# A gated cross-attention and mixture-of-experts block: a new order in the tail, and all expert numbers of a block table loaded by TensorE ahead of its blocks

## The reference

```python
def attn(q, kv, mask):                      # q = layernorm(x), kv = ctx
    qh, kh, vh = heads(q @ Wq.T), heads(kv @ Wk.T), heads(kv @ Wv.T)
    p = softmax(einsum('bhqd,bhkd->bhqk', qh, kh) + mask)
    return concat(einsum('bhqk,bhkd->bhqd', p, vh)) @ Wo.T

def ffn(x):                                 # x = layernorm(x)
    shared = (silu(x @ shared_gate.T) * (x @ shared_up.T)) @ shared_down.T
    probs = sigmoid(x @ router_w.T + routing_bias)          # 8 experts
    scores, idx = top_k(probs, 2); scores /= scores.sum(-1, keepdims=True)
    w = zeros(tokens, 8).at[idx].add(scores)
    g, u = silu(einsum('th,ehi->tei', x, gate_w)), einsum('th,ehi->tei', x, up_w)
    return shared + einsum('tei,eih,te->th', g * u, down_w, w)   # inner size 256

x = x + tanh(g_xattn) * attn(layernorm(x), ctx, mask)
x = x + tanh(g_ffn) * ffn(layernorm(x))
```

## Time and profile before

| | us |
|---|---|
| median of 3 runs | 206.19 (205.8 to 206.8) |
| the profiled execution, whole | 207.47 |
| its span, from the first to the last instruction | 204.9 |

### The profile page before, as it was taken

How to read it: one execution, slowest core, us unless ns; L and a number is a source line. 1 busy time by engine, 2 the same in 40 slices (tenths; PEclk the granted TensorE clock), 3 DMA queues, 4 the chain that set the end, 5 groups by cost and what they waited for, 6 DMA issues and landing times.

```text
span 204.9 us, 4737 instructions
## 1 busy us (share of the span) xinstructions
PE 169.0 (82%) x1400; PEld 141.6 (69%) x1400; DVE 133.6 (65%) x622; ACT 110.2 (54%) x402; POOL 110.6 (54%) x146
## 2 busy tenths in 40 slices
PE   7498798899998999989999685897498999999300
PEld 7386577888798987889987574786377776776200
DVE  2486997649895767767687686367565565665124
ACT  4368889178674586783688531435243554654100
POOL 5079889727976055784445986324314455555600
PEclk9999999999999999999999999579799999999955
DMA  5999971800000000010000100120011122131054
GB/s 154 315 385 394 353 297 41 326 0 16 2 3 13 5 0 14 30 39 3 0 0 5 41 13 13 43 62 31 28 44 52 52 69 57 43 86 34 18 151 156
DMA packets 12583, 17.35 MB, mean 85 GB/s; under 512 B 2011, under 2 KB 8929, under 8 KB 12432
## 3 DMA queue, kind: packets, MB, share of 16 engines
q1 hardware_dynamic: 10160, 14.28, 20.6%
q0 software_dynamic: 1312, 2.26, 3.8%
q10 hardware_dynamic: 1088, 0.52, 0.9%
HBM read 10.01 MB, written 7.51 MB: 85 GB/s over the span
## 4 chain that ended last, share of the span: by engine, by line
PE 54%; DVE 17%; DMA 9%; issue 7%; POOL 6%; ACT 4%; SPq 1%; ACTq 0%; POOLq 0%
PE misc L379 7%; PE o_bank L368 6%; PE s_even L343 5%; PE pt L353 4%; PE proj_k L620 4%; DVE probs L873 3%; DMA wq_raw<-wqT 3%; PE proj_q L300 3%; DMA ys<-probsT,xg 3%; POOL ys L1357 3%; PE proj_k L300 2%; DMA probs<-ys 2%; PE proj_q L302 2%; PE proj_q L301 2%; PE proj_k L302 2%
## 5 line engine op out<-in xcount | busy, mean ns | idle before, releaser
L672 ACT ACTIVATE probs<-probs,negmax 128x128 f32<-128x128 f32 x128 | 49.9, 392 | 9.1 <-DVE negmax L873 9.1
L1255 POOL TENSOR_TENSOR probs<-probs,rinv 128x512 f32<-128x512 f32 x32 | 32.9, 1040 | 28.1 <-DVE rinv L887 28.0
L1357 POOL DMA_INDIRECT ys<-probsT,xg x23 | 22.6, 983 | 25.5 <-ACT probsT L802 16.8
L672 ACT ACTIVATION_READ_ACCUMULATOR probs<-probs,negmax 128x1 f32 x128 | 24.2, 189 | 0.0
L873 DVE CUSTOM_DVE_ANT_0 probs<-s_even,mask 128x128 f32<-128x128 f32 x64 | 17.9, 279 | 4.4 <-issue 4.4
L343 PE MATMUL s_even<-kT,qT 64*128 64x128 f32 x128 | 18.4, 284 | 2.9 <-issue 2.9
L1285 POOL DMA_INDIRECT xs<-xrow,slot x16 | 16.1, 1005 | 8.1 <-issue 4.7
L620 PEld LDWEIGHTS proj_k<-down_sb,v 128*128 128x128 f32 x92 | 12.1, 190 | 10.6 <-issue 10.6
L343 PEld LDWEIGHTS s_even<-kT,qT 64*128 64x128 f32 x128 | 15.4, 187 | 5.1 <-issue 4.4
L620 PE MATMUL proj_k<-down_sb,v 128*128 x92 | 16.2, 299 | 2.9 <-DVE v L1192 2.4
L343 PE MATMUL s_odd<-kT,qT 64*128 64x128 f32 x128 | 18.5, 285 | 0.0
(11 more groups left out here) (236 smaller groups left out, 455.7 us busy)
## 6 DMA issues: line engine op xcount, KB each, us to landing
xs<-pad SPq DMA_DIRECT2D x5, 858.0 KB, 5.6
xg<-xs SPq DMA_DIRECT2D x23, 66.0 KB, 1.9
down_sb<-down SPq DMA_DIRECT2D x1, 1152.0 KB, 8.8
gu_raw<-gu SPq DMA_DIRECT2D x3, 256.0 KB, 7.0
wk_raw<-wkT SPq DMA_DIRECT2D x2, 256.0 KB, 4.7
wq_raw<-wqT SPq DMA_DIRECT2D x2, 256.0 KB, 6.7
mask<-mask SPq DMA_DIRECT2D x8, 64.0 KB, 2.2
wv_raw<-wvT SPq DMA_DIRECT2D x2, 256.0 KB, 7.1
```

Of the source, the lines that this page charges most:

```text
L672: e = act.activation(probs[:, r, l, :], probs[:, r, l, :], ACT.Exp, bias=negmax[:, r, l:l + 1], scale=-1.0, accum_out=rowsum[:, r, l:l + 1])
L1255: pool.tensor_tensor(quad, quad, rinv[:, r, 4 * u:4 * u + 4].unsqueeze(2).to_broadcast([P, 4, P]), ALU.mult).then_inc(norm_done, 1)
L1357: pool.indirect_dma_start(out=ys, out_offset=bass.IndirectOffsetOnAxis(ap=xg[n % IN_FLIGHT][:, P:P + 1].bitcast(U32), axis=0), in_=y_sb[n ...
```

## The change

It has these parts, all behind the attention of batch 5 except where a line says otherwise.

- TensorE's order: `transposes(15)` ahead of `gate_up(0, 0)`; `out_project(7)` directly behind `values(15)`, ahead of `logits(3)` and `gate_up(0, 1)`; `down_step(0)` into the first block; `gate_up(1, 0)`, `gate_up(1, 1)` into the last block and `down_step(1)` behind it.
- The block loop is cut in two, `blocks(0, EARLY)` and `blocks(EARLY, BLOCKS)`. A part ends with its last `block_down` before the next one begins. The second waits for the second table, which VectorE now makes (`table_steps(1)`) after the first block's `add_shared(0)`.
- All `block_expert` loads of a part stand at its head: five ahead of block 0, 18 ahead of block 5.
- The first half of the shared expert takes silu as tanh (`gate_tanh` on ScalarE and two operations of VectorE, `gate_hidden`).
- `choose_steps` finds the experts with `max_index`; its chain is five steps shorter to follow and has no scan.
- GpSimd splits the weights of the last experts and spreads the scatters at other places; `scatter(2)` comes ahead of `count_chosen(2)`.
- `ys` is laid out so that a token's two rows are neighbours; four loads of 256 KB take the place of eight of 128 KB, and SyncE and ScalarE store two parts each.
- PSUM banks are given out anew for this.

```diff
-        g_bank, u_bank = [s_bank[0], pt_bank[0]], [s_bank[1], pt_bank[1]]
-        d_bank = [proj_bank["k"], proj_bank["q"]]
-        route_bank = [misc, misc, proj_bank["q"], proj_bank["q"], proj_bank["q"]]
+        g_bank = [[s_bank[0], pt_bank[0]], [o_bank, s_bank[0]]]
+        u_bank = [[s_bank[1], pt_bank[1]], [misc, s_bank[1]]]
+        d_bank = [pt_bank[1], proj_bank["q"]]
+        route_bank = [misc, misc, proj_bank["q"], proj_bank["q"], proj_bank["k"]]
         x2_cols, lg_cols, rk_cols = slice(P, 3 * P), slice(384, 400), slice(400, 416)
         cnt_cols = slice(416, 424)
-        tx_bank, hT_bank, y_bank = [o_bank, misc], pt_bank, proj_bank["k"]
+        tx_bank, hT_bank, y_bank = [o_bank, misc], pt_bank[0], pt_bank[1]
...
+        y_rows = probs.rearrange("p r l k -> p (r l) k")[:, 0:B * TOP_K, :]
+
+        def load_y(engine, n):
+            part = slice(2 * TOP_K * n, 2 * TOP_K * (n + 1))
+            engine.dma_start(y_rows[:, part, :], ys.rearrange("(p r) h -> p r h", p=P)[:, part, :]).then_inc(in_y[n], 16)
+
+        def store_out(engine, n):
+            tiles = slice(2 * n, 2 * n + 2)
+            engine.wait_ge(sum_ready, n + 1)
+            engine.dma_start(out[:, tiles, :], x_sb[:, tiles, :]).then_inc(out_sem, 16)
 
...
-                load_y(sp, n, 0)
-            for n in range(4):
-                tiles = slice(2 * n, 2 * n + 2)
-                sp.wait_ge(sum_ready, n + 1)
-                sp.dma_start(out[:, tiles, :], x_sb[:, tiles, :]).then_inc(out_sem, 16)
+            load_y(sp, 0)
+            load_y(sp, 2)
+            store_out(sp, 0)
+            store_out(sp, 2)
...
             transposes(14, 2)
             out_project(B - 2, use)
             values(14, last, 2)
+            pe.wait_ge(ez_ready, 3)
             ranks(2)
+            transposes(15, 3)
             pe.wait_ge(gulo_ready, EXPERTS)
             pe.wait_ge(ttr_done, 8 * GROUPS)
             gate_up(0, 0)
-            transposes(15, 3)
             x2_transposes(3)
             values(15, last, 3)
+            out_project(B - 1, use + 1)
             logits(3)
             gate_up(0, 1)
-            out_project(B - 1, use + 1)
+            x2_transposes(LAST)
+            pe.wait_ge(ez_ready, 4)
             ranks(3)
-            pe.wait_ge(in_down, 16)
-            down_step(0)
-            x2_transposes(LAST)
             logits(LAST)
-            pe.wait_ge(h_done, 1)
-            gate_up(1, 0)
-            pe.wait_ge(h_done, 2)
-            gate_up(1, 1)
-            pe.wait_ge(ez_ready, LAST + 1)
-            ranks(LAST)
 
 
             def block_expert(n):
                 late = n >= EARLY
-                if n == 0 or n == EARLY:
-                    pe.wait_ge(table_ready, 1 + late)
                 row = n - EARLY * late
                 return pe.value_load(table[late][row:row + 1, 1:2], min_val=0, max_val=E_ROUTED)
 
...
-                    pe.wait_ge(h_done, 3)
+                    pe.wait_ge(h_done, 1)
...
-                if n >= 2:
-                    pe.wait_ge(hidT_ready, n - 1)
+                if n:
+                    pe.wait_ge(hidT_ready, n)
                 else:
-                    pe.wait_ge(h_done, 4)
+                    pe.wait_ge(h_done, 2)
                 for c in range(2):
-                    mm = pe.transpose(hT_bank[n % 2][:, c * P:(c + 1) * P], hid[n % 2][:, c * P:(c + 1) * P], ident_sb[:])
...
+            def blocks(first, end):
+
+                experts = {n: block_expert(n) for n in range(first, end)}
+                block_transpose(first)
+                block_transpose(first + 1)
+                block_gate_up(first, experts[first])
+                for n in range(first, end):
+                    if n + 2 < end:
+                        block_transpose(n + 2)
+                    if n + 1 < end:
+                        block_gate_up(n + 1, experts[n + 1])
+                    if n == BLOCKS - 1:
+                        pe.wait_ge(xglo_ready, BLOCKS)
+                        gate_up(1, 0)
+                    if n > first:
+                        block_down(n - 1, experts.pop(n - 1))
+                    elif not first:
+                        pe.wait_ge(in_down, 16)
+                        down_step(0)
+                    block_hidden_transpose(n)
+                    if n == BLOCKS - 1:
+                        pe.wait_ge(hid_ready, BLOCKS)
+                        gate_up(1, 1)
+                block_down(end - 1, experts[end - 1])
+
+            pe.wait_ge(ez_ready, LAST + 1)
+            ranks(LAST)
+            pe.wait_ge(table_ready, 1)
+            blocks(0, EARLY)
+            pe.wait_ge(table_ready, 2)
+            blocks(EARLY, BLOCKS)
+            pe.wait_ge(counts_read, 2)
+            down_step(1)
...
+            def gate_tanh(c):
+                act.wait_ge(gu_done, c + 1)
+                act.activation(silu_sb[:, c, :], g_bank[0][c][:], ACT.Tanh, scale=0.5).then_inc(silu_done, 1)
+
+            def silu(c):
+                act.wait_ge(gu_done, c + 3)
+                act.wait_ge(h_done, c + 1)
+                act.activation(silu_sb[:, c, :], g_bank[1][c][:], ACT.Silu).then_inc(silu_done, 1)
...
+                    if n == BLOCKS - 1:
+                        silu(0)
+                block_y(end - 1)
+
+            blocks(0, EARLY)
+            blocks(EARLY, BLOCKS)
+            silu(1)
             for i in range(IN_FLIGHT):
                 act.wait_ge(y_out[i], 16 * len(range(i, BLOCKS, IN_FLIGHT)))
-            for n in range(4):
-                load_y(act, n, 1)
+            load_y(act, 1)
+            load_y(act, 3)
+            store_out(act, 1)
+            store_out(act, 3)
...
+                for i, b in enumerate(ROUTED[r]):
+                    dve.max_index(chosen_at[:, b, :], top[:, b, :], prob[:, i, :]).then_inc(route_step, 1)
...
+            def gate_hidden(c):
+                dve.wait_ge(silu_done, c + 1)
+                dve.scalar_tensor_tensor(silu_sb[:, c, :], silu_sb[:, c, :], 1.0, g_bank[0][c][:], ALU.add, ALU.mult).then_inc(gate_done, 1)
+                dve.wait_ge(gate_done, c + 1)
+                dve.scalar_tensor_tensor(h_sb[:, 0, c, :], silu_sb[:, c, :], 0.5, u_bank[0][c][:], ALU.mult, ALU.mult).then_inc(h_done, 1)
+
+            def hidden(c):
+                dve.wait_ge(silu_done, c + 3)
+                dve.tensor_tensor(h_sb[:, 1, c, :], silu_sb[:, c, :], u_bank[1][c][:], ALU.mult).then_inc(h_done, 1)
...
-            mask_max(15, PAIRS - 1, 3, after(6, copy_o, 13, 1))
-            x2_lo(2)
+            mask_max(15, PAIRS - 1, 3, chain(after(2, x2_lo, 2), after(5, copy_o, 13, 1)))
             recips(15, 3, (0,))
             copy_pt(14, 2)
-            finish(choose_steps(2))
+            choice = choose_steps(2)
+            run(choice, 3)
             recips(15, 3, (1,))
+            finish(choice)
             add_attention(B - 2, use)
+            norm = norm2_steps(B - 2, use)
+            run(norm, 2)
+            finish(weight_steps(2))
             copy_o(14, 2)
-            steps = norm2_steps(B - 2, use)
-            run(steps, 2)
-            finish(weight_steps(2))
             place(2)
-            block_table(0)
+            first_table = table_steps(0)
+            run(first_table, 1)
             copy_pt(15, 3)
-            finish(steps)
+            finish(norm)
             copy_o(15, 3)
             x2_lo(3)
-            hidden(0, 0, 0)
-            finish(choose_steps(3))
-            hidden(1, 0, 1)
+            finish(first_table)
             add_attention(B - 1, use + 1)
-            steps = norm2_steps(B - 1, use + 1)
-            run(steps, 2)
+            norm = norm2_steps(B - 1, use + 1)
+            run(norm, 2)
+            choice = choose_steps(3)
+            run(choice, 4)
+            finish(norm)
+            finish(choice)
             finish(weight_steps(3))
-            finish(steps)
+            x2_lo(LAST)
             place(3)
-            x2_lo(LAST)
-            add_shared(0)
+            gate_hidden(0)
             finish(choose_steps(LAST))
             finish(weight_steps(LAST))
-            hidden(2, 1, 0)
-            place(LAST)
-            hidden(3, 1, 1)
-            block_table(1)
 
             def block_lo(n):
                 dve.wait_ge(xghi_ready, n + 1)
...
+            def blocks(first, end):
+
+                block_lo(first)
+                block_lo(first + 1)
+                if not first:
+                    place(LAST)
+                    gate_hidden(1)
+                block_hidden(first)
+                for n in range(first, end):
+                    if n > first:
+                        block_hidT(n - 1)
+                    if n + 2 < end:
+                        block_lo(n + 2)
+                    if n + 1 < end:
+                        block_hidden(n + 1)
+                    if n == 0:
+                        add_shared(0)
+                        finish(table_steps(1))
+                    if n == BLOCKS - 1:
```

(84 more changed lines are left out.)

105 lines of the change are left out of this document (29 added, 76 removed).

## The result

The changed kernel takes 215.84 us in the median of four runs (214.11 to 217.28), the kernel before 206.5 in the same comparison. The ratio is 1.046, with a 95% interval of 1.036 to 1.056: slower. Ratios leave out executions that took over 1.5% longer than the fastest one of their kernel, while medians, as the 206.5 with its one of 209.54, keep them. The forecast was 214.6. The profiled execution took 215.86 us with a span of 214.1.

What follows compares the result with a forecast made beforehand. Bound in the block loop by a TensorE-VectorE cycle (1.53 us) and, close by, TensorE's sequencer with its loads. +9.5 - 2.3 + 2.2 - 1.0 = +8.4 on the profiled 207.47 gives 215.9, against the median 214.6 us; range 208.5 to 219.0.

Steps and rivals of the forecast that it cites:

- The price of a bare load: One load of an expert number on TensorE when nothing covers it: 0.64 us, bounds 0.47 and 0.70.
- SyncE's rhythm: Five loads of the same kind on SyncE, each with a DMA issue, 1.10 us each, so nothing overlapped.
- The rival of overlapped loads: On TensorE consecutive loads overlap, some 0.12 us each, 2.8 for all 23: 202.7 us, faster; chance 0.10.
- Item 1: Way to the last routing round: earlier reciprocal, split and out-projection bring the last ranks about 8 us forward.
- (d): Before the last ranks: gate_up(0, 1) adds 0.6 to 1.3, gate_hidden(0) 1.4; shorter choice saves 0.4, moved gate_up(1, ...) 0.8.
- Item 2: Head of block 0: five loads on the path with TensorE's queue empty, 5 x 0.64 = 3.2 us.
- Item 3: Block 0's gate product is held only by rounding and remainder, 1.2 us: at 139.6, 6.9 earlier.
- Item 4: Blocks 0 to 4: 8.2 to the first down product plus 4 x 1.53, together 14.3 us.
- Item 5: Ahead of block 5: 18 loads, 11.5 us, then the loop refills at half clock, 5.6; its down product +9.5.
- Item 6: The 17 steps from block 5 to block 22: 1.62 us each, 27.5 for 29.8, -2.3 (bounds 0 and -3.8).
- Item 7: Last two blocks: gate_up(1, 0) and hidden(0) delay block 22's down product by 2.2 us (bounds 1.2 and 3).
- Item 8: The end: four loads of neighbouring rows for eight of scattered ones win 1.0 us (at most 2, at least 0).

## Why the prediction held, step by step

- **The price of a bare load** (0.64 forecast): 0.653 in three kernels. It was read from one load's start and end, and from SyncE's rhythm, which said that such loads don't overlap. The three kernels are the changed one, that with nine loads ahead and that in the old order. By the rule of the Trainium skill ("DMA: Bandwidth & Descriptors", section "Latency and other measured facts") the floor of some 600 ns agrees; of the amortizing that it mentions, 18 loads in a row show nothing. Loads without bounds started 0.37 us apart, below that floor. The rival of overlapped loads is out.
- **Item 1, the way to the last round** (-8, bounds -5 and -9): -9.5, outside its bound. The out-projection started at 125.23 in place of 132.74, 7.5 us earlier, where 3.5 + 3.9 = 7.4 were forecast. It ran at full clock, 2.07 us for 3.25, a gain of 1.2; I had counted 0.7 and then most of 1 more, so the clock is not what was missed. The step that failed is (d), with the choice and the gate products behind it: I had put +1.2 for the way from the out-projection to the last ranks, and it came out at -0.85 (6.22 us for 7.07). gate_up(0, 1) ahead of the last x2 transpose cost nothing (+1.0 forecast), since it ran while the transpose had to wait for the layer norm anyway, and `gate_hidden(0)` held up the last choice by 0.5 us and not by 1.4. The choice (-0.4) and the gate products (-0.9) came out about as forecast. No run tests these parts one by one.
- **Item 2** (3.2): 3.35 idle. **Item 3** (1.2 from transpose to gate product): 1.22. **Item 4** (14.3 to block 4's down product): 14.6.
- **Item 5** (11.5 for the loads and 5.6 for the refill): 11.37 and 5.70. Of the refill 1.2 to 1.5 us are the clock's: it took 4.53 with one load a block and 4.16 with matmuls between the loads, both at a granted clock of 1.00. That the cut costs 4.0 by itself: 5.55 - 1.61 = 3.9 where it stands, of which the loop in one piece gave back 2.1 with eight buffers.
- **Item 6** (27.5 with a step of 1.62): the first 15 steps took 24.7, 1.65 each, with one wait of 1.6 us for rows. That the loads' removal is worth 0.08 a block was right only with ten buffers; with eight it brought 0.2 us in all.
- **Item 7** (+2.2): the last two steps took 4.85 for 3.06, +1.8.
- **Item 8** (-1.0) was wrong: from the last write's issue to the end 11.5 us before and 11.8 now. Before, the first sum began 5.2 us behind that issue, and the sums waited once (0.8); now it begins 6.4 behind it and they don't wait, so that they take 3.3 us and not 4.2. The sums are the gain that I had counted; I had given the first landing no delay, and it was 1.2. Eight loads for four changed nothing (6.42 us against 6.33), so it isn't the size of a load; whether the new layout of rows or something else delays the first landing stays open.

Items 1 and 8 missed in opposite directions (-1.5 and +1.3), so the sum came out nearer than its parts. That the forecast for the profiled execution, 215.9, met its 215.86 is luck: its span grew by 9.2 us and not 8.4, and 0.8 of that came back outside the span, where the kernel before spends 2.6 us and the changed one 1.8.

## What to carry to other kernels

Here, loading a register from memory was work of TensorE's sequencer, in order and one at a time: 0.653 us each. One behind queued matmuls is nearly free (0.08 us a block); a batch ahead of the work is bare, and stops the engine and everything that feeds on it (11.37 us for 18). Look where the engine has work queued, and put one load there for each use; and count what idle time does to the clock behind it (1.2 to 1.5 us here). Removing something small from a loop brings little while another cycle, here a ring of buffers, has no slack (0.2 us in place of 1.2): lengthen that first.

## What the runs showed of the hardware that I had not expected

- A load with bounds took 0.653 us, one without 0.37, but without bounds each later use of the number cost steps of 37 and 173 ns and a check of 18 in place of 46 ns, and the loop's step went from 1.53 to 2.05 us. In this kernel bounds are cheaper at the load.
- Four loads of 256 KB and eight of 128 KB, in the new layout of rows, let the first sum begin at the same time, 4.1 and 4.2 us behind the first issue (190.30 to 194.37, 191.43 to 195.59). The eight loads of the kernel before, in the old layout, needed 2.9 (195.62 to 198.56).
